# Cross attention and a quantised feed-forward block on one core: the first layer norm's statistics of two token groups computed on ScalarE instead of VectorE

## The reference

```python
x = x + xattn(layernorm(x), ctx, Wq, Wkv)     # x: 2 x 2048 x 512, ctx: 2 x 128 x 512
x = x + ffn(layernorm(x), w_gate, w_up, w_down)
# layernorm: (x - mean(x)) / sqrt(var(x) + 1e-5) over the 512 features of a token
# xattn: softmax((q Wq)(c Wk)^T / sqrt(512)) (c Wv), one head
# ffn: every activation is rounded to 16 bits with one scale for the whole tensor
#      (its largest magnitude / 32767), the weights to 4 bits with a scale per 32:
#      x = qdq(x); up = qdq(x Wu^T); gate = qdq(x Wg^T)
#      o = qdq(qdq(gate * sigmoid(gate)) * up); return o Wd^T
```

## Time and profile before

| | us |
|---|---|
| median of 3 runs | 923.49 |
| lowest, highest | 919.52, 924.36 |
| profiled execution, as a run | 919.46 |
| its span in the profile | 917.7 |
| busy: TensorE / VectorE / ScalarE / GpSimd | 877.0 / 658.9 / 567.1 / 146.0 |

### The profile page before, as it was taken

One profiled execution on the slowest core, in us unless ns is written; L12 is line 12 of the kernel. 1 busy time (PEld: TensorE's weight loads), 2 busy tenths in 40 slices (PEclk: granted clock), 3 DMA queues, 4 the chain that ended last, 5 costly groups with the idle time before them and its releaser, 6 DMA issues.

```text
span 917.7 us, 12146 instructions
## 1 busy us (share of the span) xinstructions
PE 877.0 (96%) x4308; PEld 440.2 (48%) x4308; DVE 658.9 (72%) x951; ACT 567.1 (62%) x693; POOL 146.0 (16%) x110
## 2 busy tenths in 40 slices
PE   7999889999999999999999979999799988999997
PEld 5788664444444444444444434444344433444443
DVE  4999896732436243279987679766799988979792
ACT  2379887543544454499986777942789965535420
POOL 0199940075003910000000000000000000000000
PEclk9999999999999999999999999999799999999999
DMA  9722217334369559963449984799977888989862
GB/s 341 323 93 93 108 77 263 149 151 159 139 250 285 209 169 318 319 266 138 161 166 340 323 337 160 283 391 377 400 257 266 280 309 308 390 290 341 302 248 92
DMA packets 92031, 226.57 MB, mean 247 GB/s; under 512 B 31952, under 2 KB 31952, under 8 KB 89808
## 3 DMA queue, kind: packets, MB, share of 16 engines
q1 hardware_dynamic: 90832, 221.80, 67.1%
q10 hardware_dynamic: 1152, 4.19, 1.2%
HBM read 127.40 MB, written 92.27 MB: 239 GB/s over the span
## 4 chain that ended last, share of the span: by engine, by line
PE 64%; DVE 11%; DMA 9%; issue 6%; POOL 5%; ACT 4%; SPq 1%; DVEq 0%; ACTq 0%; POOLq 0%
PE ps L828 27%; PE ps L861 18%; PE ps L906 12%; PE ps L923 4%; DVE big L1521 3%; DVE big L1514 3%; DMA big<-in_L_ffn_w_gate_dram 2%; DMA up_park<-big 2%; DMA big<-gate_park 2%; POOL big L666 2%; ACT big L941 1%; PE ps L701 1%; DMA first_park<-big 1%; POOL big L650 1%; POOL big L656 1%
## 5 line engine op out<-in xcount | busy, mean ns | idle before, releaser
L941 ACT ACTIVATE big<-ps 128x1024 f32<-128x1024 f32 (+2 forms) x194 | 153.8, 814 | 208.9 <-PE ps L828 102.7
L861 PE MATMUL ps<-big 128*128 (+1 forms) x1152 | 250.8, 381 | 4.7 <-ACT big L941 4.7
L828 PE MATMUL ps<-big 128*128 (+1 forms) x1152 | 248.8, 379 | 0.3 <-DVE big L1393 0.3
L861 PEld LDWEIGHTS ps<-big 128*128 128x128 f16 x1152 | 112.8, 98 | 142.6 <-issue 6.1
L828 PEld LDWEIGHTS ps<-big 128*128 128x128 f16 x1152 | 112.5, 98 | 136.3 <-DVE big L1393 0.8
L1411 DVE TENSOR_REDUCE small<-big 128x1 f32<-128x1024 f32 (+1 forms) x48 | 58.3, 1219 | 135.9 <-ACT big L941 135.8
L906 PE MATMUL ps<-big 128*128 128x512 f16 x576 | 127.0, 383 | 5.7 <-DVE big L1542 5.7
L906 PEld LDWEIGHTS ps<-big 128*128 128x128 f16 x576 | 56.6, 99 | 75.5 <-issue 5.1
L887 PE MATMUL ps<-big 128*128 128x512 f16 x384 | 85.3, 384 | 7.1 <-ACT big L1148 7.1
L642 POOL PARTITION_ALL_REDUCE small<-small x9 | 3.6, 411 | 534.5 <-DVE small L1490 183.9
L1443 DVE TENSOR_REDUCE small<-big 128x1 f32<-128x1024 f32 x48 | 58.2, 1215 | 12.8 <-ACT big L941 12.8
(11 more groups left out here) (100 smaller groups left out, 995.8 us busy)
## 6 DMA issues: line engine op xcount, KB each, us to landing
big<-up_park SPq DMA_DIRECT2D x90, 512.0 KB, 5.6
up_park<-big SPq DMA_DIRECT2D x48, 512.0 KB, 4.7
gate_park<-big SPq DMA_DIRECT2D x42, 512.0 KB, 2.7
big<-gate_park SPq DMA_DIRECT2D x42, 512.0 KB, 6.0
sign_park<-big SPq DMA_DIRECT2D x48, 256.0 KB, 2.2
big<-in_x_dram SPq DMA_DIRECT2D x8, 1024.0 KB, 18.0
x_park<-big SPq DMA_DIRECT2D x8, 1024.0 KB, 3.9
product_park<-big SPq DMA_DIRECT2D x16, 512.0 KB, 4.5
```

The costliest lines, as they stand in the source:

```text
L828: mm = nc.tensor.matmul(ps[:, 2 * (n % 2) + j], w[:, a, k, o:o + P], XT[:, g, b, k], start=(k == 0 and a + b == 0), stop=(k == KC - 1 and ...
L861: mm = nc.tensor.matmul(ps[:, b + j], WU[:, a, k, o:o + P], XT[:, g, c, k], start=(k == 0 and a + c == 0), stop=(k == KC - 1 and c == 1))
L941: return nc.scalar.activation(dst, src, ACT.Copy)
```

## The change

The statistics of groups 2 and 3 are computed by ScalarE in two passes. In n = 0 and 1 (group 2; n = 4 and 5 for group 3) it makes two copies with a sum each (`sum1`), VectorE turns the four sums into negated means at n = 2 (n = 6) with `mean1`, ScalarE squares the centred tiles with a sum in n = 2 and 3 (6 and 7), two each (`spread1`), and VectorE turns the four sums into a variance at n = 4 (n = 8) with `spread_var1`. All land ahead of the exponentials in ScalarE's list. `stats1` and `var1` remain for groups 0, 1 and 4 to 7. Semaphore counts of the second norm are shifted by the eight squares and two means; the constant -0.5 is set by VectorE among the first constants. The line numbers behind the change are larger by 2 to 39.

```diff
+ACT_STATS = (2, 3)
+N_SQ = TI * len(ACT_STATS)
...
         def _(pool):
-            nc.gpsimd.memset(half, -0.5).then_inc(half_d, 1)
-            pool.wait_ge(half_d, 1)
+            pool.wait_ge(consts, 5)
...
             def spread(n):
-                act.wait_ge(negm_d, n + 1)
-                need(act, ssq_d, n)
+                act.wait_ge(negm_d, len(ACT_STATS) + n + 1)
+                act.wait_ge(ssq_d, N_SQ + n)
...
+            def sum1(m):
+                n = TI * ACT_STATS[0] + m
+                act.wait_ge(x_ld[n // TI], 16)
+                need(act, sum1_d, m)
+                need(act, ssq_d, m // TI * TI)
+                nc.scalar.activation(squares, X[:, n // TI, n % TI], ACT.Copy, accum_out=xsum[:, n:n + 1]).then_inc(sum1_d, 1)
+
+            def spread1(m):
+                n = TI * ACT_STATS[0] + m
+                act.wait_ge(negm_d, m // TI + 1)
+                act.wait_ge(sum1_d, m // TI * TI + TI)
+                need(act, ssq_d, m)
+                nc.scalar.activation(squares, X[:, n // TI, n % TI], ACT.Square, bias=negm[:, n:n + 1],
+                                     accum_out=ssq[:, n:n + 1]).then_inc(ssq_d, 1)
...
                     take_xT(n + 1)
+                if n < N_SQ:
+                    for m in range(n // TI * TI + n % 2 * 2, n // TI * TI + n % 2 * 2 + 2):
+                        if n % TI < 2:
+                            sum1(m)
+                        else:
+                            spread1(m)
...
+            nc.vector.memset(half, -0.5).then_inc(consts, 1)
...
+            def mean1(g):
+                c = slice(TI * g, TI * g + TI)
+                dve.wait_ge(sum1_d, TI * (ACT_STATS.index(g) + 1))
+                nc.vector.tensor_scalar(negm[:, c], xsum[:, c], -1.0 / D, None, ALU.mult).then_inc(negm_d, 1)
+
+            def spread_var1(g):
+                c = slice(TI * g, TI * g + TI)
+                dve.wait_ge(ssq_d, TI * (ACT_STATS.index(g) + 1))
+                nc.vector.tensor_scalar(ve1[:, c], ssq[:, c], 1.0 / D, EPS, ALU.mult, ALU.add).then_inc(ve1_d, 1)
...
-                if n + 2 * TI < NT:
+                if n < N_SQ:
+                    if n % TI == 2:
+                        mean1(n // TI + 2)
+                if n in (TI, N_SQ):
+                    spread_var1(n // TI + 1)
+                if N_SQ <= n and n + 2 * TI < NT:
                     stats1(n + 2 * TI)
```

More of the change, by code:

```diff
@@ L293, in build @@
         wn_ld = {m: sem(f"wn_ld{m}") for m in (1, 2)}
-        consts, half_d = sem("consts"), sem("half_d")
+        consts, sum1_d = sem("consts"), sem("sum1_d")
         pro_mm, pro_ev, pro_c = sem("pro_mm"), sem("pro_ev"), sem("pro_c")
@@ L701, in turn @@
                 return nc.tensor.transpose(dst, src, ident)
-            pe.wait_ge(consts, 4)
+            pe.wait_ge(consts, 5)
             pe.wait_ge(ctx_ld, 16)
@@ L1258, in var1 @@
             def var1(g):
-                dve.wait_ge(bn1_d, TI * g + TI)
+                dve.wait_ge(bn1_d, TI * g + TI - (N_SQ if g > ACT_STATS[-1] else 0))
                 for i in range(TI):
                     nc.vector.bn_aggr(mv[:, i], bn[:, TI * g + i]).then_inc(mv1_d, 1)
-                dve.wait_ge(mv1_d, TI * g + TI)
+                dve.wait_ge(mv1_d, TI * g + TI - (N_SQ if g > ACT_STATS[-1] else 0))
                 nc.vector.tensor_scalar(ve1[:, TI * g:TI * g + TI], mv[:, 0:TI, 1], EPS, None,
                                         ALU.add).then_inc(ve1_d, 1)
+            def mean1(g):
[6 more added lines that the diff above has]
+                nc.vector.tensor_scalar(ve1[:, c], ssq[:, c], 1.0 / D, EPS, ALU.mult, ALU.add).then_inc(ve1_d, 1)
             def score_max(g):
@@ L1301, in var2 @@
                 c = slice(TI * g, TI * g + TI)
-                dve.wait_ge(ssq_d, TI * g + TI)
+                dve.wait_ge(ssq_d, N_SQ + TI * g + TI)
                 nc.vector.tensor_scalar(ve[:, c], ssq[:, c], 1.0 / D, EPS, ALU.mult, ALU.add).then_inc(ve2_d, 1)
```

## The result

| | before | changed |
|---|---|---|
| median, us | 923.53 (21 runs) | 930.66 (21 runs) |
| lowest, highest, us | 917.96, 931.76 | 927.54, 934.11 |
| profiled execution, as a run / its span | 919.46 / 917.7 | 932.64 / 930.8 |

The ratio of the changed kernel to the one before is 1.0069, 95% interval [1.0053, 1.0085]: by it the changed kernel is 6.4 us slower (0.0069 x 923.5), where 3.3 was forecast.

A forecast was written before the change was run, and what follows sets the result against it. From 48 on nearly full engines couldn't make up lost time; ScalarE's added 11.7 us exceeded its 6.7 idle, making attend(0) 3.5 and GpSimd 2.9 to 3.5 late. Taken as +3.3 on the median 923.49: 926.8, range 922 to 931.

The forecast's parts named there:

- The bound and the side: First stage: ScalarE's added passes exceed its idle time, ScalarE without idle time from 35 to 50; end 3.3 us later.
- the relief: VectorE, n = 0 to 7: about 6 us of statistics work leaves it, counted at nothing for the end.
- the sum: Whole forecast: +3.3 us at the gate product and the end, giving 926.8 on the median.
- the wait on oneself: Second of each ScalarE pair starts 0.04 us after the first's end; sum 0.75 instead of 0.60, square 0.86 instead of 0.71.
- the sum itself: ScalarE's copy with a sum, n = 0, 1, 4, 5: 0.60 us each without waiting for its predecessor.
- the square: ScalarE's centred square with a sum, n = 2, 3, 6, 7: 0.71 us each without waiting for its predecessor.
- Rival 1, the clock: TensorE's clock falls in the new wait before attend(0): 1.3 to 2.0 us more, 928.1 to 928.8; chance 0.23.
- The 0.6 us that VectorE was to get back: Before the variance, VectorE's small multiply (0.81 us at 58.49) comes when GpSimd is out of work, taking 0.23.
- So the delay stays: After attend(0), 3.5 us late, TensorE runs without a pause, so the delay persists; GpSimd stays late by 2.9 to 3.5.
- the later stages shift the end by the same amount: From the gate product on: whatever the first stage loses or gains moves the end equally, +3.3 us at both.

The follow-up runs named there:

- e2: Changed kernel without the sixteen ScalarE passes and the means, variance of groups 2 and 3 a constant 1.0; ratio to the kernel before 0.9986.
- e1: Kernel before with the sixteen ScalarE passes added, results unused, VectorE keeping all its work; ratio 1.0044, 927.23 us against 923.99.
- e4: Changed kernel with a scratch tile for each token tile, so no ScalarE pass waits for the one ahead; ratio to the kernel before 1.0051.
- e3: Changed kernel with ten unused 128x128 matmuls on TensorE in n = 6, just before and into the new wait; ratio to the kernel before 1.0058.
- the second trace: Changed kernel unedited, profiled once more; 933.47 us as a run.
- e12: Changed kernel with one unused 0.19 us multiply on GpSimd ahead of its quantisation part, to restore the distance; ratio to the kernel before 1.0057.
- e11: e6 with VectorE quantising the first of eight parts of the weights at n = 4 in place of GpSimd; ratio to the kernel before 1.0025.
- e9: Kernel before with one unused 0.35 us reduction on VectorE ahead of the reciprocals of group 2; ratio 1.0030.
- e6: Changed kernel with both groups' ScalarE passes moved to where ScalarE waits anyway; ratio to the kernel before 1.0000.
- e5: Changed kernel with only group 2 on ScalarE, VectorE doing group 3 with bn_stats; ratio to the kernel before 0.9997.

## Why the prediction was right or wrong

**The bound and the side: right.** ScalarE's queue became the limit of n = 0 to 7, no exponential waits for VectorE, the relief is worth nothing (e2) because GpSimd is busy to 62, and the load alone gives the slowdown (e1: 4.1 us, forecast 3.3). The median of 930.66 lies inside the range of 922 to 931, but only 0.3 us from its end. That it does is in part luck: the sum left out the collision and made the wait on oneself too small, and the gate product, forecast 3.3 us late, is 7.2 and 9.8 us late in the two traces, of which the stages behind it gave some back.

**The wait on oneself: mis-sized.** I put the second of each pair 0.04 us behind the accumulator read, after a row of two ACTIVATEs without one. It is 0.10. Seven pairs stand ahead of the copy of P^T: 0.4 us; the sum itself (0.61 against 0.60) and the square were right. That makes the copy of P^T 4.7 us late instead of 4.24, and 4.76 was measured. e4, without the waits, has attend(0) 1.1 us sooner than the changed kernel.

**Rival 1, the clock: in part.** It fell in the very place, to 0.72 between 48 and 54 in both traces. I had priced it at 1.3 to 2.0 us on top; e3 shows 0.3 us at attend(0) and nothing at the gate product. At the full clock TensorE has 0.87 us to spare ahead of attend(0) and waits for the low half of P, so most of what the fall costs is hidden. Over all timed runs the mean granted clock is 0.9863 in the changed kernel, 0.9885 in e3 and 0.9872 in the one before, so by an estimate the clock explains about 0.001 of the run, a microsecond. Together with the waits it makes attend(0) 4.3 to 4.45 us late instead of 3.5.

**The 0.6 us that VectorE was to get back: right for the multiply that I named, but half of the picture.** The multiply of 0.81 us at 58.49 is that of group 1. In the changed kernel it came at 64.53, beside an idle GpSimd, and took 0.23, as forecast. But the multiply of group 0, which I left as it was, came at 54.87, when GpSimd was still quantising, and took 1.46. In sum nothing came back: from attend(0) to the first normalisation are 14.55 us, before 14.57. In the second trace, where the multiply of group 0 took 0.81 us, they are 13.94, and in e3 and e12 too. So the 0.6 us hang on a few tenths in the start of another small instruction, and the first normalisation is 4.4 and 3.7 us late in the two traces, where I had 2.9 to 3.5.

I had the right row, and read from it a price (0.81 beside GpSimd, 0.23 alone) where it is a matter of when the multiply starts: where it starts inside one of GpSimd's long instructions it ends with that one (54.87 + 1.46 = 56.33 against 54.82 + 1.48 = 56.30). The Trainium skill ("SBUF — State Buffer", "SBUF: two separate sides") says this: VectorE and GpSimd share a port pair; an instruction of GpSimd's, or one of VectorE's of certain kinds, holds it to its end if it starts first, while the other is blocked. The traces agree as to the whole instruction, with 0.23 us alone, and 0.81, 1.26, 1.46, 1.47 and 1.53 beside instructions of 0.83 and 1.48 us, and e11 shows GpSimd held in its turn. They don't agree if "first" goes by the start times that the trace gives: at 73.18 VectorE's starts 0.03 us ahead, and it is the one that is held.

**"So the delay stays": wrong, and the step that failed.** From 48 on I shifted everything alike, and the term for what happens between there and the gate product was nothing. But VectorE and GpSimd are late by different amounts. Counted from the second copy of the loop, GpSimd's multiply of the weights in group 2 comes at +37.57 instead of +33.12, so 4.45 us late, and VectorE's small one at +37.54 instead of +32.76, 4.78 late. These 0.33 us put it from 0.36 us ahead of GpSimd's instruction to 0.03 us ahead, and there it is caught. The kernel before stands 0.36 to 0.43 us clear of this in three groups running. Where it is caught, n0 to n4 is 1.5 us longer and n4 to n7 2.1, in the changed kernel's second trace as in e9, which has none of the change. By itself a slow multiply needn't cost anything: e6 has it at 1.46 us in group 0 and is no slower. That it costs more in groups 2 to 4 because VectorE and GpSimd are both nearly full there fits the busy times, but no run shows it by itself.

**The sum.** ScalarE's load is 4.1 us by e1 and 4.7 by e4, both without the collision in groups 2 to 4; the changed kernel is 6.4. The 1.7 to 2.3 us between fit the collision (2.8 us in e9), though in the profiled executions of e1 and e4 the clock fell at 110, and n4 to n7 is 1.4 and 1.7 us longer there; it is so in e2 and e5 too (1.2 and 1.4), which are no slower than the kernel before in the timed runs, so that fall belongs to single executions. The intervals of these ratios overlap, and the two runs meant to take the collision out of the changed kernel moved it instead. That it costs time is shown; how much of the 6.4 us is its share is not settled. Nor is why the gate product is late by more than the end: 7.2 and 9.8 us in the two traces of the changed kernel, against 6.4 in the timed runs. It is the same in nine of the ten variants (e3 7.2 us against 5.4, e9 6.2 against 2.8; only e11 has 1.9 against 2.3), so the assumption that the later stages shift the end by the same amount isn't borne out by these numbers, though each gate product is that of one execution or two. What these stages take varied between 780 and 788 us over all the traces, the two kernels unedited included (781.5 and 786.3 before, 783.7 and 787.6 changed), with no order in it that I could find.

## What to carry to other kernels

An engine's idle time isn't room for work until you have laid the work into its queue: half of the passes, or all of them in other places, cost nothing that could be measured, and the same passes ahead of one copy that another engine waits for cost 4 us. Where VectorE and GpSimd both work in on-chip memory, don't price a small instruction by its mean; look at the distance between its start and the start of the other engine's long instruction, since a few tenths of a microsecond decide between 0.23 and 1.5 us; then ask whether anyone waits for it, since in group 0 of e6 nobody lost by the 1.46 us. And a kernel whose engines run in step can stand just clear of such a meeting, so a shift "of everything alike" has to be tested at each place where two delays differ.

## What the runs showed of the hardware that was not expected

- A 128x4 multiply on VectorE takes 0.23 us alone and up to 1.53 us if it starts just before or inside a two-input 128x768 multiply of GpSimd; at 0.36 us ahead it is free, at 0.03 us ahead it is not (both in e4). The limit isn't the same for every small instruction: the 128x4 one that gives the mean in the changed kernel starts 0.01 us ahead of GpSimd's of 1.49 us (48.52 and 48.53) and takes 0.17, as when it is free.
- It goes the other way too: a two-input 128x768 multiply of GpSimd takes 2.20 us instead of 1.47 where it starts 0.10 us behind one of VectorE's (e11).
- An ACTIVATE that waits for the semaphore of the one ahead, with a sum, starts 0.10 us behind that one's accumulator read; from start to start 0.81 us instead of 0.61 for a 128x512 sum.
- A wait of 2.0 us with little work around it was followed by a mean granted clock of TensorE of 0.72 over 6 us (48 to 54), yet ten filler matmuls, with which it stayed at 1.00, bought only 0.3 us at attend(0).
